# Second expert layer: weighted outputs added to the residual by the scatter instead of in the last stage

## The reference

```python
x = layernorm(x + L1_attn(x))                     # residual of the last part
logits = x @ Wg
top_v, top_i = top_k(logits, 2)
top_w = softmax(top_v)                            # of two: 0.5 +- 0.5 tanh((v1 - v2) / 2)
y_e = (silu(x @ W1[e]) * (x @ W3[e])) @ W2[e]     # for the two experts e in top_i
out = layernorm(x + top_w[0] * y_0 + top_w[1] * y_1)
```

## Time and profile before

| | |
|---|---|
| median of 3 runs | 1515.99 us (1512.83 to 1517.7) |
| profiled execution, first to last instruction | 1624.0 us |
| PE busy | 1309.6 us (81%) |
| DVE, ACT, POOL busy | 1042.4 us (64%), 780.3 us (48%), 733.0 us (45%) |
| DMA | 101.78 MB, mean 63 GB/s |
| mean granted TensorE clock | 0.912 |

### The profile page before, as it was taken

How to read it: one execution, slowest core, us unless ns; L and a number is a source line. 1 busy time by engine, 2 the same in 40 slices (tenths; PEclk the granted TensorE clock), 3 DMA queues, 4 the chain that set the end, 5 groups by cost and what they waited for, 6 DMA issues and landing times. The chain is left out here.

```text
span 1624.0 us, 32890 instructions
## 1 busy us (share of the span) xinstructions
PE 1309.6 (81%) x9154; PEld 1124.0 (69%) x9155; DVE 1042.4 (64%) x3450; ACT 780.3 (48%) x1557; POOL 733.0 (45%) x1079
## 2 busy tenths in 40 slices
PE   3999898897187877839999999999469999999910
PEld 2887777776177777726766666666369999999900
DVE  1788778777355555525877776776646666666548
ACT  1454445443154554415545454544145555555547
POOL 0034453354457676720234343434535555555556
PEclk9999999998599999958999998999679999999955
DMA  6111111100222222232212110200121111111155
GB/s 201 33 51 48 40 37 31 55 26 27 67 70 78 75 74 76 65 99 66 72 53 87 31 47 31 71 20 27 41 68 55 54 55 53 54 55 52 40 157 164
DMA packets 124804, 101.78 MB, mean 63 GB/s; under 512 B 15234, under 2 KB 111106, under 8 KB 124290
## 3 DMA queue, kind: packets, MB, share of 16 engines
q1 hardware_dynamic: 97010, 59.98, 13.3%
q0 software_dynamic: 17408, 35.82, 6.2%
q10 hardware_dynamic: 10320, 5.19, 1.1%
HBM read 60.96 MB, written 44.20 MB: 65 GB/s over the span
## 5 line engine op out<-in xcount | busy, mean ns | idle before, releaser
L954 POOL DMA_INDIRECT expert_out<-e_ysb,e_idx x288 | 302.6, 1051 | 102.4 <-issue 97.7
L1111 PE MATMUL bank<-w_dn,e_h 128*128 x1728 | 222.9, 279 | 51.5 <-DVE e_h L1072 41.6
L1101 PE MATMUL bank<-e_x_hi,e_w_hi 128*128 128x256 f32 x864 | 259.5, 300 | 0.1
L1111 PEld LDWEIGHTS bank<-w_dn,e_h 128*128 128x128 f32 x1728 | 207.7, 194 | 59.2 <-issue 58.8
L1101 PE MATMUL bank<-e_x_lo,e_w_hi 128*128 128x256 f32 x864 | 246.7, 286 | 0.0
L1101 PE MATMUL bank<-e_x_hi,e_w_lo 128*128 128x256 f32 x864 | 246.6, 285 | 0.0
L1072 DVE TENSOR_TENSOR e_h<-bank,e_sgl 128x512 f32<-128x512 f32 x216 | 149.0, 690 | 150.5 <-PE bank L1101 101.8
L980 ACT ACTIVATE e_sgl<-bank 128x512 f32<-128x512 f32 x216 | 129.2, 598 | 143.3 <-PE bank L1101 104.1
L1101 PEld LDWEIGHTS bank<-e_x_hi,e_w_hi 128*128 128x128 f32 x864 | 167.7, 194 | 0.4 <-issue 0.3
L1101 PEld LDWEIGHTS bank<-e_x_lo,e_w_hi 128*128 128x128 f32 x864 | 167.9, 194 | 0.0
L1101 PEld LDWEIGHTS bank<-e_x_hi,e_w_lo 128*128 128x128 f32 x864 | 167.7, 194 | 0.0
(11 more groups left out here) (261 smaller groups left out, 2745.7 us busy)
## 6 DMA issues: line engine op xcount, KB each, us to landing
e_xg<-scattered SPq DMA_DIRECT2D x144, 129.0 KB, 2.1
b_cy<-expert_out SPq DMA_DIRECT2D x32, 256.0 KB, 3.1
f_cy<-expert_out SPq DMA_DIRECT2D x32, 256.0 KB, 2.9
expert_out<-e_ysb,e_idx POOLq DMA_INDIRECT x288
a_xb<-in_x SPq DMA_DIRECT2D x16, 256.0 KB
out<-f_x ACTq DMA_DIRECT2D x16, 256.0 KB, 2.3
scattered<-in_spare SPq DMA_DIRECT2D x2, 1032.0 KB
scattered<-in_spare SPq DMA_DIRECT2D x16, 129.0 KB
```

The lines of the kernel that those rows point to most:

```text
L954: nc.gpsimd.indirect_dma_start(out=expert_out, out_offset=bass.IndirectOffsetOnAxis(ap=idx[d.slot][:, i:i + 1], axis=0), in_=ysb[d.slot][: ...
L1101: mm = nc.tensor.matmul(banks[bank_of(j, c)][:, i * ROWS:(i + 1) * ROWS], w_[c.slot][:, g, f:f + P], x_[c.slot][:], start=(k == 0), stop=( ...
L1111: mm = nc.tensor.matmul(YB[d.odd][:, i * D:(i + 1) * D], h[d.odd][:, f, i * P:(i + 1) * P], w_dn[:, bass.ds(e, 1), f, :].rearrange("p o d ...
```

## The change

- The rows in `scattered` get one column more (`WIDE` 130), which holds the weight of the token's choice in layer 2. The router of retention 1 computes it: DVE subtracts the two logits (`dif`), ACT takes the tanh at the end of its step (`tanh_of`), POOL writes 0.5 +- 0.5 tanh into the row in `put_places`, which now waits for the tanh. The copies to `logits` and `top_l` fall away there, and the pieces between the first steps of `experts(1)`.
- ACT no longer copies the residual to `xres` but stores it to a new DRAM buffer `sums`, from where the scatter adds to it.
- In `experts(1)` DVE copies the weights of the step's rows to `wt`, and ACT evicts in two instructions, each scaled by a column of `wt`. POOL's two indirect DMAs carry `compute_op=ALU.add` and go to `sums`. Two DMAs may add to the same token's row, so POOL waits, ahead of each step's mark, until the DMAs of the step before have landed. The two DMAs within a step hold different tokens.
- `finish` loads `sums` (one load of 256 KB a sequence), DVE takes the statistics, POOL works out variance, power and bias, ACT applies the norm and stores.

```diff
@@ Router
+            def tanh_of(self, act, t):
+                act.wait_ge(self.dif_there, t.n + 1)
+                wait_count(act, self.places, TOPK * (t.n - 1))
+                nc.scalar.activation(self.th[t.odd][:], self.dif[t.odd][:], ACT.Tanh, scale=0.5).then_inc(self.th_there, 1)
 
             def put_places(self, pool, t):
                 wait_count(pool, self.sent[t.odd], SCATTERS * t.half)
+                if self.weighted:
+                    pool.wait_ge(self.th_there, t.n + 1)
                 for k in range(TOPK):
...
+                    if self.weighted:
+                        place = nc.gpsimd.tensor_scalar(
+                            self.x[k][t.odd][:, :, D + 1:WIDE].rearrange("p c o -> p (c o)"), self.th[t.odd][:],
+                            (0.5, -0.5)[k], 0.5, ALU.mult, ALU.add)
@@ experts, GpSimd
                             wait_count(pool, marked, d.n)
+                            if layer:
+                                wait_count(pool, st[(d.slot - 1) % 4], SENT * (d.quarter + (d.slot > 0)))
                             wait_apart(pool, 2 + d.odd).then_inc(marked, 1)
                             for i in range(ROWS // P):
                                 nc.gpsimd.indirect_dma_start(
-                                    out=expert_out, out_offset=bass.IndirectOffsetOnAxis(
+                                    out=sums if layer else expert_out, compute_op=ALU.add if layer else ALU.bypass,
+                                    out_offset=bass.IndirectOffsetOnAxis(
@@ experts, ScalarE
-                            nc.scalar.copy(ysb[d.slot][:], YB[d.odd][:, 0:ROWS].rearrange("p (r d) -> p r d", d=D)
-                                           ).then_inc(y_there, 1)
+                            if layer:
+                                act.wait_ge(wt_there, d.n + 1)
+                                for i in range(ROWS // P):
+                                    last_i = nc.scalar.activation(
+                                        ysb[d.slot][:, i, :], YB[d.odd][:, i * D:(i + 1) * D], ACT.Copy,
+                                        scale=wt[:, bass.ds(d.n, 1), i:i + 1].rearrange("p o i -> p (o i)"))
+                                last_i.then_inc(y_there, 1)
@@ retention1, ScalarE
-                            nc.scalar.copy(xres[:, bass.ds(d.n * CH, CH), :], x3[d.odd][:, :, 0:D]).then_inc(x3_kept, 1)
+                            act.dma_start(sums_seq[:, bass.ds(d.n, 1)].rearrange("p b c d -> p (b c) d"),
+                                          x3[d.odd][:, :, 0:D]).then_inc(x3_kept[d.odd], 16)
...
                             comb.norm.apply(act, comb.r[y.odd], xb[y.odd], y, x2_there)
+                        if d:
+                            router.tanh_of(act, d)
@@ finish, GpSimd
+                            pool.wait_ge(mv_there, c.n + 1)
+                            wait_count(pool, x4_there, c.n - 3)
...
+                            L(nc.gpsimd.tensor_tensor(ve[c.slot][:], mv[c.slot][:, :, 1], c_eps[:], ALU.add))
+                            L(nc.gpsimd.tensor_tensor(rstd[c.slot][:], ve[c.slot][:], c_half[:, 0:CH], ALU.pow))
+                            L(nc.gpsimd.tensor_tensor(minus[c.slot][:], rstd[c.slot][:], c_neg[:], ALU.mult))
+                            ch_pw.end()
+                            nc.gpsimd.tensor_tensor(bias[c.slot][:], mv[c.slot][:, :, 0], minus[c.slot][:], ALU.mult
+                                                    ).then_inc(bias_there, 1)
```

More of the change, by code:

```diff
@@ L142, in load_expert @@
             sp.dma_start(w_dn[:, e, 0:f // P, :], dn[e].rearrange("(j p) d -> p j d", p=P)).then_inc(sem, 16)
+        sent_sems = [[whole.enter_context(nc.semaphore(f"sent{l}{i}")) for i in range(2)] for l in range(2)]
+        st_sems = [[whole.enter_context(nc.semaphore(f"st{l}{i}")) for i in range(4)] for l in range(2)]
         used = []
@@ L537, in _ @@
                     nc.gpsimd.memset(c_zero[:], 0).then_inc(s_cset, 1)
+                    router.clear_weights(pool)
                     pool.wait_ge(s_cset, 3)
@@ L905, in experts @@
                 ld = [sem(f"ld{i}") for i in range(4)]
-                st = [sem(f"st{i}") for i in range(4)]
+                st = st_sems[layer]
                 x_mm, x_hi_there, x_ev = sem("x_mm"), sem("x_hi_there"), sem("x_ev")
@@ L1170, in add @@
                 self.add_second(dve, t)
-            def scale_first(self, act, t, done):
-                self.wait_loaded(act, t)
-                y, w = self.y[self.slot(t)], self.wt[self.slot(t)]
-                for c in range(CH):
-                    last = nc.scalar.activation(y[:, c, :], y[:, c, :], ACT.Copy, scale=w[:, c:c + 1])
-                last.then_inc(done, 1)
-            def add_first(self, pool, t, scaled, done):
-                pool.wait_ge(scaled, t.n + 1)
-                nc.gpsimd.tensor_tensor(self.r[self.slot(t)][:], self.y[self.slot(t)][:, 0:CH, :],
-                                        xres[:, bass.ds(t.n * CH, CH), :], ALU.add).then_inc(done, 1)
             def add_second(self, dve, t):
@@ L1357, in _ @@
                     run_steps(act, first, last, SEQS, lags, body)
+                    for i in range(2):
+                        act.wait_ge(x3_kept[i], 16 * SEQS // 2)
                 @block.vector
@@ L1573, in finish, with _, body @@
                 block = ph.enter_context(nc.Block())
+                @block.sync
+                def _(sp):
+                    def body(ts):
+                        a = ts[0]
+                        if a:
+                            wait_count(sp, x4_there, a.n - 3)
+                            sp.dma_start(r[a.slot][:], sums_seq[:, bass.ds(a.n, 1)].rearrange("p b c d -> p (b c) d")
+                                         ).then_inc(got[a.slot], 16)
+                    run_steps(sp, first, last, SEQS, [0], body, unroll=4)
+                @block.vector
+                def _(dve):
+                    def body(ts):
+                        b = ts[1]
+                        if b:
+                            dve.wait_ge(got[b.slot], 16 * b.quarter + 16)
+                            wait_count(dve, mv_there, b.n - 1)
+                            ch_st.start(dve, b)
+                            for c in range(CH):
+                                last_i = nc.vector.bn_stats(stats[b.odd][:, c, :], r[b.slot][:, c, :])
+                            ch_st.link(last_i)
+                            ch_st.end()
+                            wait_count(dve, bias_there, b.n - 3)
+                            wait_apart(dve)
+                            for c in range(CH):
+                                last_i = nc.vector.bn_aggr(mv[b.slot][:, c, :], stats[b.odd][:, c, :])
+                            last_i.then_inc(mv_there, 1)
+                    run_steps(dve, first, last, SEQS, lags, body, unroll=4)
                 @block.gpsimd
```

140 lines of the change are left out of this document (78 added, 62 removed).

## The result

| | before | after |
|---|---|---|
| median (lowest to highest), same chip | 1514.82 us (1512.83 to 1517.7) | 1572.14 us (1571.6 to 1574.14) |
| ratio to before, 95% interval | | 1.0368 (1.0336 to 1.04), +57.3 us |
| profiled execution, first to last instruction | 1624.0 us | 1570.8 us |

The kernel became slower by more than twice the +24.7 us forecast; the time lies inside the range, at what rival (b) gave (1570). Experts 1 and finish take the same time on both kinds of chip (343.9 us from the first issue to the last on either with plain scatters and no wait; finish 66.9 to 68.1 on one, 67.8 on the other), so their differences can be read from the two traces.

The account below looks back on a forecast made before the run. PE was taken to bound experts 1 and ACT to end last in finish. Adding and wait +42.9, finish -21, end of retention 1 +3.5 and pieces -0.7 gave +24.7 us: 1541, range 1499 to 1592.

Parts of the forecast that it names:

- rival (b): Experts 1: the added read costs as much as the existing one, e = 1.3, +53.5 us, 1570; chance 0.20.
- The chained step, 4.5 us: Experts 1: mark to mark through two issues and the landing takes 4.5 us without adding cost, against PE's 4.88.
- e: Experts 1: adding's cost per step, twice one issue's growth plus the landing's growth; forecast 0.9 us, high end 1.6.
- the crossing at 0.36: Experts 1: PE stays the bound up to e = 0.36, where the lines of drain cost and chained steps cross.
- 72e - 21.9: Experts 1: change in us when all 72 steps are chained; +42.9 at e = 0.9.
- Finish was forecast at -21: Finish: one load, no scaling or additions, step 2.25 us instead of 3.34, ACT still last; -21 us (-17 to -23).
- The end of retention 1: Retention 1's drain: last scatter waits for the tanh behind ACT's norm, plus small POOL operations; +3.5 us (+2 to +5).
- The pieces, -0.7: Start of experts 1: a tanh and a few DVE operations between the first steps fall away; -0.7 us.
- The middle of retention 1, forecast zero: Retention 1: store's issue replaces a similar copy on ACT, DVE loses a tiny copy; zero, without PE's cover -2 to +3.
- (a): Experts 1: the adding lands within the slack, PE stays the bound, -14.4 us, 1502; chance 0.20.
- (c): Finish doesn't shorten, stores and four slots holding its step at 3.3 us; adds 17, 1558 with e = 0.9; chance 0.05.
- (d): Experts 1: the add is far slower, each row read and written in turn, e above 1.6, over 1591; chance 0.08.

Follow-up runs that it names:

- wait alone: Kernel before with only the new wait for the previous step's landing in experts 1, plain scatters: 1624.47 us, ratio 1.0004.
- none adds: Changed kernel with plain scatters, the wait kept, and ACT's tanh moved ahead of the two norms: 1500.48 us, ratio 0.9895.
- first adds: Kernel before with the new wait, only the first of each step's two scatters in experts 1 adding: 1528.55 us, ratio 1.0082.
- second adds: Kernel before with the new wait, only the second of each step's two scatters in experts 1 adding: 1663.45 us, ratio 1.0238.
- both add: The changed kernel itself, with the wait and both scatters of a step adding: 1572.14 us, ratio 1.0368.
- first two groups: Follow-up runs on two chips, where the kernel before takes 1623.15 us and 1624.59 us.
- sum in finish: Changed kernel with plain scatters to rows of their own, no wait, xres kept, finish adding both results; 1618.91 us (tanh early), 1511.15 us (tanh late).
- third group: Follow-up runs on a chip where the kernel before takes 1516.57 us.
- the add alone: Kernel before with only compute_op=ALU.add on the scatters of experts 1, no new wait: 1626.63 us, ratio 1.0024.
- run 51: Not a run's number: 51 counts marks in the kernel before with only the new wait, plain scatters: 1624.47 us, ratio 1.0004.

## Why the prediction was wrong, point by point

**The chained step, 4.5 us: right as a sum of before's pieces, but not the length at which a plain chain ran.** The path from mark to mark, each piece a mean over 52 middle steps of the timeline (landing: last semaphore count of the second scatter, after its issue's end). "Chain" is the sum of the pieces, with 0.1 from landing to mark also where the mark waited for something else; "step" is what was measured between marks:

| us | mark to issue | first issue | gap | second issue | to landing | to mark | chain | step |
|---|---|---|---|---|---|---|---|---|
| before (no wait) | 0.67 | 0.98 | 0.34 | 1.16 | 1.26 | (0.1) | 4.5 | 4.88 (PE) |
| wait alone | 0.95 | 1.19 | 0.33 | 0.97 | 1.33 | 0.1 | 4.9 | 4.88 |
| none adds (changed kernel, tanh early) | 0.68 | 1.00 | 0.34 | 1.11 | 1.28 | (0.1) | 4.5 | 4.90 (PE) |
| first adds | 0.63 | 1.60 | 0.30 | 0.99 | 1.27 | 0.1 | 4.9 | 4.90 |
| second adds | 0.51 | 1.00 | 0.32 | 1.58 | 1.76 | 0.1 | 5.3 | 5.29 |
| both add | 0.51 | 1.58 | 0.30 | 1.55 | 1.71 | 0.1 | 5.8 | 5.77 |

The landing, put at 1.3 us behind the issue's end, measured 1.26 to 1.33 with plain scatters; one reading on the way to it was off (the load's packets end at 1349.0 in the earlier trace rows, not 1349.2) without harm. The 4.5 depends on what else runs: with the wait alone the mark or the first issue was held up by a DVE instruction (hardware section) and the chain grew to PE's step, and in the stage's last steps it took 4.36 us, with a second issue of 0.97 instead of 1.16. The wait costs nothing more than the drain in either case.

**e, the adding: the step that failed.** The mechanism (a chain from landing to next issue that outgrows PE's step) was right; the term for the adding was sized too small, and within it the growth of the two issues. The sum took a quarter more for each issue (0.5 in all) and 0.4 on the landing, e = 0.9. An issue grew by 0.58 and 0.44, 1.02 in all, and the landing by 0.43; the path from mark to issue gave back 0.17. Chain against chain that is 5.77 - 4.50, so **e = 1.3**. The landing was sized right, the issues' growth at half of what it is. Rival (b) had the issues right, on the ground that 128 rows take about 1 us in both kinds of scatter; it was given the smaller chance on the ground that a part of an issue must be fixed. Neither ground was tested, since every scatter here has 128 rows. Since 72 steps multiply it, 0.4 us too little on e is 29 of the 33 us between forecast and time. e depends on the plain chain that it is measured from: it is 1.6 in the stage's last steps (5.9 us against 4.36), where no plain issue is held up by DVE and each issue grows by 0.6, and 0.9 against the 4.9 of the wait alone, whose chain had filled its slack. What the time goes by is the step, and that was 5.77 for the 5.4 forecast.

**PE as a bound while e is small: as forecast, though the crossing at 0.36 itself wasn't measured.** With none adding the wait costs +4.0 and +4.1 us in experts 1, for the chained drain that was put at +3.8; with the first alone adding the chain is 4.9 us in the middle steps, level with PE, and 5.0 in the stage's last steps (+12 us in the time); with the second alone or both, the step is the chain, and every tenth of a us counts 72-fold.

**The stages.** 72 x (4.5 + e) and 72e - 21.9 with e = 1.3 give +71.7; from the first issue of experts 1 to finish's first load measured 421.9 us for 349.2, +72.7. Finish was forecast at -21 and is -20.7 (46.2 from its first load for 66.9). The end of retention 1, forecast at +3.5: from the last norm's power to the first load of experts 1 are 33.3 us, for 30.6 with before's retention 1 on a chip of the same kind (first-adds run), +2.7; the moved tanh gave 4.4 with all of the stage. As a whole, though, retention 1 takes 447.5 us in that first-adds run, with before's code and in an execution 6.7 us over the run's median, and 447.7 in the changed kernel, so what the change costs there is known to a few us only. The pieces, -0.7, don't show: from the first load of experts 1 to its first issue are 18.5 us for 18.4. In all +72.7 - 20.7 + 2.7 to 4.4 makes +54.7 to +56.4, for +57.3 measured, which is as near as these stages can be read across executions.

**The middle of retention 1, forecast zero: not so on one kind of chip.** On the chips of the first two groups the stage, from its first load to that of experts 1, takes 494.1 and 495.3 us in the two kernels with store and late tanh, 481.0 with copy and early tanh, and 476.4 to 481.2 with before's. Two of them, in the same columns as above:

```profile
696.80:1195.60 498.80, 414.60 (x2322) 304.04 (x2322) 324.67 (x1392) 219.11 (x435) 180.47 (x272) 0.85 0.21 62
```

(changed kernel with plain scatters), and with the sum in finish:

```profile
706.80:1191.30 484.50, 398.10 (x2322) 287.93 (x2322) 325.43 (x1392) 225.98 (x450) 177.65 (x272) 0.89 0.18 55
```

PE is busy 16 us longer for the same 2322 multiplications, with 0.85 of its clock granted instead of 0.89. Whether the store, the late tanh or both bring that about there stays open: the runs meant to tell them apart came to a chip where the 14 us are absent.

**The rivals.** (a) fell with e. (b) happened in size (e = 1.3, step 5.8, 1570) and nearly in its parts: it had 1.0 on the issues, 1.02 measured, and 0.3 on the landing, 0.43 measured, less the 0.17 given back. Its cause, a second read for each row, isn't shown by that. The sentence of the Trainium skill cited beside it (Collectives: The Full Stack, on the two source reads of an add) points the same way in its result, a slower transfer; the trace shows the cost on the issue and in the number of packets, and no second read in the bytes counted (35.95 MB in POOL's queue and 56.94 MB read from HBM, with and without the adding). (c) and (d) didn't occur. The wait that the Trainium skill asks for (DMA: Bandwidth & Descriptors, Rules for kernel authors) costs 4 us of experts 1 without the add, and 66 us of the time with it (1692.69 against 1626.63).

## What to carry to other kernels

When an issue has to wait for the landing of the transfer before it, everything between becomes a chain: add it up (gap, issues, landing) and hold the sum against the step of the engine that bounds. While the sum is under that step, the chain costs only its drain; once it is over, every step pays. The pieces of such a sum can change with what they run beside: here a shift in time put POOL's mark into a long DVE instruction and ate the slack. When one term of such a chain is unknown and is multiplied by 72, and no row of the trace has it, a small run that measures it (here: the add alone, with its issues of 1.57 us) is worth more than a choice between two guesses. The gain that could be had was a small one and needed no adding: weights applied at the eviction, plain scatters and no wait, -5.7 and -5.4 us.

## What the runs showed of the hardware

- **An adding scatter is a different transfer from a plain one.** The page's queue of POOL's DMAs, changed kernel and then the same with plain scatters and the early tanh (packets, MB, share of the 16 engines' span):

```profile
q0 software_dynamic: 33536, 35.95, 11.2%
```

```profile
q0 software_dynamic: 17408, 35.95, 6.7%
```

Its burst takes 0.9 us for 0.3, its issue 1.54 to 1.60 us for a mean of 1.0 to 1.2, with or without a wait. That the packets are why the issue is longer is likely, and wasn't tested.
- **The instruction behind an adding issue starts inside it.** `idx` starts 0.99 us into the 1.54 of the issue and takes 0.79 instead of 0.20, so its end, 0.24 us behind the issue's, is about where it would have been.
- **A mark of one element took 0.95 to 1.05 us instead of 0.18** in three of four steps of the run with the wait alone, and 0.40 in the first-adds run. In the fourth the mark took 0.18 and the first issue 1.87. The marks were ended by the DMA, though ACT had been ready for 1.4 us, and the step was still 4.88:

```profile
1341.17 1.05 POOL L172 TENSOR_TENSOR mark<-c_half 1x1 f32<-1x1 f32 x1 [1.20 <-DMA expert_out<-e_ysb,e_idx]
1342.37 0.99 POOL L956 DMA_INDIRECT expert_out<-e_ysb,e_idx  x1 [0.15 <-POOL mark L172]
```

  The trace tells what it coincides with. DVE splits weights with one instruction of 1.23 us a step:

```profile
1340.94 1.23 DVE L1064 TENSOR_TENSOR e_w_lo<-w_gu,e_w_hi 128x1024 fp32r<-128x1024 f32 x1 [0.31 <-ACT e_w_hi L973]
```

  Of the 72 marks of that run 51 start while it runs, and all 51 end 0.04 to 0.05 us after it; the other 21 take 0.18. A plain issue that starts while it runs ends 0.84 to 0.86 us after it, and takes up to 1.43 us in the kernel before (66 of 144 issues, all others 0.99 or less) and up to 1.87 with the wait alone. Behind the last `w_lo` no mark and no issue is long. No run moved that instruction, so this is shown by the times alone.
- **Two kinds of chip.** The same code up to the end of retention 1, on the chip of before's trace and on that of the third group (columns as above, the stages retention 0, experts 0, retention 1):

```profile
0.00:437.00 437.00, 352.42 (x2224) 289.32 (x2225) 303.69 (x1125) 176.67 (x339) 163.37 (x215) 0.94 0.19 56
437.00:704.20 267.20, 202.87 (x1584) 193.86 (x1584) 136.31 (x297) 128.36 (x294) 175.20 (x288) 0.94 0.24 71
704.20:1188.80 484.60, 400.15 (x2322) 287.54 (x2322) 325.58 (x1408) 224.75 (x434) 172.76 (x240) 0.88 0.18 55
```

```profile
0.00:402.10 402.10, 339.37 (x2224) 286.06 (x2225) 303.16 (x1125) 178.19 (x339) 163.52 (x215) 0.93 0.21 61
402.10:632.80 230.70, 199.79 (x1584) 190.50 (x1584) 132.07 (x297) 135.19 (x294) 174.52 (x288) 0.95 0.28 83
632.80:1083.80 451.00, 382.36 (x2322) 280.12 (x2322) 325.77 (x1408) 225.15 (x434) 173.23 (x240) 0.90 0.20 59
```

  The stages are 35, 37 and 34 us longer on the first; DVE is as busy on both (304 and 303 us, 326 and 326), PE busy 13, 3 and 18 us longer, and the granted clock differs by 0.02 at most, so neither busy time nor clock explains the rest. The 108 us don't come from the profiler: timed runs on the chips of the first two groups take 1623 to 1625 us too, and those on the third 1517. That it is the chip, and not something else that differed between these sets of runs, is the likeliest reading; no run tells them apart. The ratio of the change was the same on both (1.0368 and 1.0358).
